# Second layer in three sets instead of two, expert results added on VectorE, one product for features and logits, all orders written anew

## The reference, cut to what matters

```python
# layer 0
f = xn @ W.T + b                                  # features, per batch of 256 tokens
e = f @ f.T + distance_bias;  s = softmax(e) @ f
shared = (silu(xn @ Sg.T) * (xn @ Su.T)) @ Sd.T
probs = sigmoid(xn @ router.T + routing_bias)     # 8 experts, the best 2 per token, weights normalised
g = shared + sum over 2 experts of weight * ((silu(xn @ G[e]) * (xn @ U[e])) @ D[e])
x = x + s * silu(g)
# layer 1
w = xn @ Wqkv.T, 16 heads of 8;  w_normed = w / norm over tokens
Pi = softmax over heads(sum(w_normed^2) * temp);  dots = sum over tokens(Pi_norm * w * w)
s = -(w * Pi / (1 + dots)) @ Wout.T + bout
expert of a batch = argmax(softmax(gelu(last token @ Wp1 + bp1) @ Wp2 + bp2))
g = xn + 0.3 * ((gelu(xn @ W1[sel] + b1) @ W2[sel] + b2) @ Wo + bo)
x = x + s * silu(g)
```

## Time and profile before

| | |
|---|---|
| median of 3 runs | 431.0 us (427.37 to 431.69) |
| profiled execution, span | 338.1 us |
| around the span (median less span) | 92.9 us |
| TensorE busy | 312.5 us, 92% of the span |
| TensorE weight loads | 259.6 us, 77% |
| VectorE busy | 208.9 us, 62% |
| ScalarE busy | 206.7 us, 61% |
| POOL busy | 138.5 us, 41% |
| bytes moved | 31.91 MB, mean 94 GB/s |

### The profile page before, as it was taken

One profiled execution on the slowest core, in us unless ns is written; L12 is line 12 of the kernel. 1 busy time (PEld: TensorE's weight loads), 2 busy tenths in 40 slices (PEclk: granted clock), 3 DMA queues, 4 the chain that ended last, 5 costly groups with the idle time before them and its releaser, 6 DMA issues.

```text
span 338.1 us, 7770 instructions
## 1 busy us (share of the span) xinstructions
PE 312.5 (92%) x2077; PEld 259.6 (77%) x2077; DVE 208.9 (62%) x779; ACT 206.7 (61%) x504; POOL 138.5 (41%) x152
## 2 busy tenths in 40 slices
PE   7879999999999799999998899898879999989994
PEld 6657555669999799999988767688854588768793
DVE  4999792225776765556544457665365848578465
ACT  2296754348776666565654435674586768897772
POOL 2200577777777746666664434454540000000000
PEclk9999999999999999999999999999997999999999
DMA  6980023113431113333333721111006532017403
GB/s 187 294 367 4 32 66 104 56 49 87 105 95 57 48 33 89 94 92 87 103 94 108 261 65 35 55 33 33 31 7 244 120 77 57 3 32 211 133 17 109
DMA packets 29321, 31.91 MB, mean 94 GB/s; under 512 B 7120, under 2 KB 22610, under 8 KB 29152
## 3 DMA queue, kind: packets, MB, share of 16 engines
q1 hardware_dynamic: 24960, 22.97, 24.1%
q0 software_dynamic: 4320, 8.47, 7.5%
HBM read 19.86 MB, written 12.01 MB: 94 GB/s over the span
## 4 chain that ended last, share of the span: by engine, by line
PE 72%; DVE 11%; ACT 5%; issue 5%; SPq 2%; DMA 2%; DVEq 1%; ACTq 0%
PE PS L474 19%; PE PS L486 9%; PE PS L414 4%; PE PS L690 3%; PE PS L401 3%; PE PS L440 3%; PE PS L698 3%; PE PS L626 2%; PE PS L390 2%; PE PS L392 2%; PE PS L627 2%; PE PS L642 2%; PE PS L628 2%; DVE XA L924 2%; PE PS L454 2%
## 5 line engine op out<-in xcount | busy, mean ns | idle before, releaser
L2010 POOL DMA_INDIRECT yc_scratch<-YS,XS x71 | 71.6, 1009 | 61.1 <-ACT YS L1609 44.6
L474 PE MATMUL PS<-XG,XT 128*128 128x128 f32 x568 | 76.7, 278 | 6.9 <-issue 3.0
L474 PEld LDWEIGHTS PS<-XG,XT 128*128 128x128 f32 x568 | 69.0, 192 | 10.1 <-issue 6.3
L1126 DVE COPY XT<-WE 128x512 f32 x71 | 30.9, 435 | 38.5 <-issue 21.3
L1602 ACT ACTIVATE EP<-PS 128x256 f32<-128x256 f32 x71 | 27.0, 383 | 43.3 <-PE PS L474 42.3
L486 PE MATMUL PS<-WE,EP 128*128 x284 | 43.9, 278 | 1.9 <-ACT YS L1609 1.8
L2001 POOL DMA_INDIRECT xs_scratch<-XA,POS x32 | 31.4, 981 | 29.9 <-DVE POS L1035 20.5
L486 PEld LDWEIGHTS PS<-WE,EP 128*128 128x128 f32 x284 | 37.6, 191 | 5.9 <-issue 5.9
L1117 DVE TENSOR_TENSOR EP<-EP,PS 128x256 f32<-128x256 f32 x71 | 29.6, 417 | 18.4 <-PE PS L486 15.9
L2001 POOL DMA_INDIRECT xs_scratch<-XB,POS x32 | 31.2, 976 | 9.8 <-issue 9.8
L1609 ACT ACTIVATE YS<-PS,XS 128x128 f32<-128x128 f32 x71 | 26.0, 366 | 5.2 <-PE PS L486 2.0
(11 more groups left out here) (190 smaller groups left out, 601.3 us busy)
## 6 DMA issues: line engine op xcount, KB each, us to landing
XS<-xs_scratch SPq DMA_DIRECT2D x71, 65.0 KB, 1.9
XB<-yc_scratch SPq DMA_DIRECT2D x16, 256.0 KB, 4.4
S<-in_w SPq DMA_DIRECT2D x13, 256.0 KB, 2.6
WE<-in_we SPq DMA_DIRECT2D x1, 3072.0 KB, 14.8
X<-in_x SPq DMA_DIRECT2D x16, 128.0 KB, 3.0
out<-X SPq DMA_DIRECT2D x16, 128.0 KB, 1.8
yc_scratch<-YS,XS POOLq DMA_INDIRECT x71, 2.3
SH<-in_w SPq DMA_DIRECT2D x3, 256.0 KB, 2.5
```

Source lines behind the costliest of these rows:

```text
L474: m = e.matmul(PS[k][:, f * 128:(f + 1) * 128], WC[:, u % 4, f * 128:(f + 1) * 128], XG[:, g % 2, j * 128:(j + 1) * 128], start=True, stop ...
L1126: e.tensor_copy(WC[:, u % 4, :], WE[:, bass.ds(r, 512)]).then_inc(s_wc, 1)
L2010: e.indirect_dma_start(out=yc, out_offset=bass.IndirectOffsetOnAxis(ap=XS[:, g % 4, j, 128:129].bitcast(U32), axis=0), in_=YS[:, u % 8, :] ...
```

## The change

It does six things.

1. **Routing and sets.** Group 0 is three chunks instead of four (CA = 3). The units come in three sets, for chunks 0 to 2, 3 to 5 and 6 to 7 (SETS = 0, 3, 6, 8), with a table of five runs of eight experts instead of three. The number of units stays 71. Results are collected chunk by chunk in one transfer each, and the experts of layer 1 are chosen in three sets.
2. **Results on VectorE.** `add_up` goes. `add_results` adds the two results of a chunk into F, `add_shared` adds the shared output; `gated` then reads and writes F.
3. **Features and logits in one product.** `project`, `logits` and `bias` go. `features` multiplies XT of each tile (as weights) with W and the router side by side, 136 columns; VectorE adds both biases at once into F. `turn_f` transposes F to FT.
4. **Banks per product.** Every helper of TensorE gets its bank and the semaphore value that frees it as arguments, call by call.
5. **Buffers.** HHE gets its own memory, layer 1's transposed input goes to the memory of SH (X1T), H1 and PXP to XT's.
6. **All orders anew.** The lists of SyncE, TensorE, VectorE and ScalarE are different throughout. Units 0 and 1 now start before most of the attention of layer 0; mix(13) to (15) come between units 38 and 48, layer 1 of the first set from unit 38 on. The loads of x and the stores are one transfer per chunk instead of two, and the first fetch waits for the empty rows' blocks too.

```diff
-CA = 4
+CA = 3
 NTS = (4 * CA, NT - 4 * CA)
-FULL = 8 * CA - 7
-DONE = 8 * CA + 7
-BESIDE = 36
+SETS = (0, 3, 6, 8)
+FULL = 8 * SETS[1] - 7
+DONES = (8 * SETS[1] + 7, 8 * SETS[2] + 7, NU)
...
+                if u == 0:
+                    e.wait_ge(s_experts, 1)
+                    e.wait_ge(d_fill, 16 * (NE + 1))
+                    e.wait_ge(d_disp[0], 16 * 2 * NTS[0])
+                if u == FULL:
+                    e.wait_ge(d_disp[1], 16 * 2 * NTS[1])
...
+            def collect(c):
+                if c in SETS:
+
+                    last = DONES[set_of(c)]
+                    for u in range(last - 8, last):
+                        e.wait_ge(d_y[u % 8], 16 * (u // 8 + 1))
+                if c >= 3:
+                    e.wait_ge(s_ya, c - 2)
+                e.dma_start(YC[:, 4 * (c % 3):4 * (c % 3) + 4, :, :].rearrange("p (b t) s d -> p b (t s d)", b=2),
+                            yc.rearrange("(c b p q) d -> c p b (q d)", c=NC, b=2, q=4)[c]).then_inc(d_yt[c], 16)
...
+            def features(b, k, free=None, n=0):
+
+                e.wait_ge(s_xt, b // 2 + 1)
+                if b == 0:
                     e.wait_ge(d_wa, 16)
-                for t in range(4 * c, 4 * c + 4):
-                    m = e.matmul(PS[(2, 7)[g]][:, 8 * t:8 * t + 8], tile(XT, t), a_("router"), start=True, stop=True)
...
+                when(free, n)
+                for i in range(2):
+                    m = e.matmul(PS[k][:, i * 136:(i + 1) * 136], tile(XT, 2 * b + i), WA[:, 0:136], start=True, stop=True)
+                m.then_inc(p_fl, 1)
...
-            def gate_up(u):
+            def gate_up(u, k, free=None, n=0):
                 g, j = divmod(u, 4)
-                k = u % 3 if u < BESIDE else u % 2
...
-                if u >= BESIDE:
-                    e.wait_ge(s_hhe, u - 1)
...
-            def down_e(u):
-                k = (5, 7)[u % 2] if u < BESIDE else 5
+            def down_e(u, k, free=None, n=0):
                 e.wait_ge(s_hhe, u + 1)
-                if u == 0:
-                    e.wait_ge(s_s, NB)
-                elif u >= 2:
-                    e.wait_ge(s_ys, u - 1 if u < BESIDE else u)
+                when(free, n)
...
-                e.matmul(quarters(k), ident, four(SH, c), start=True, stop=False)
-                e.matmul(quarters(k), ident, results(c, 0), start=False, stop=False)
-                e.matmul(quarters(k), ident, results(c, 1), start=False, stop=True).then_inc(p_acc, 1)
...
+            def add_results(c):
+                e.wait_ge(d_yt[c], 16)
+                e.wait_ge(p_mix, 2 * c + 2)
+                e.tensor_tensor(four(F, c), results(c, 0), results(c, 1), ALU.add).then_inc(s_ya, 1)
+
+            def add_shared(c):
+                e.wait_ge(s_sh, c + 1)
+                e.wait_ge(s_ya, c + 1)
+                e.tensor_tensor(four(F, c), four(F, c), four(SH, c), ALU.add).then_inc(s_acc, 1)
...
+            def features(b, k):
+                e.wait_ge(p_fl, b + 1)
+                if b == 0:
+                    e.wait_ge(d_wa, 16)
+                e.tensor_tensor(F[:, 2 * b:2 * b + 2, :], PS[k][:, 0:272].rearrange("p (i d) -> p i d", i=2),
+                                a_("bias").unsqueeze(1).broadcast_to([128, 2, 136]), ALU.add).then_inc(s_f, 1)
```

More of the change, by code:

```diff
@@ L42 @@
 CW, _c = {}, 0
-for _n, _w in [("ident", 128), ("one", 1), ("upper", 128), ("e8", 256), ("unit", 1), ("head", 16), ("lb", 25), ("next", 24), ("dist", 512)]:
+for _n, _w in [("ident", 128), ("one", 1), ("upper", 128), ("e8", 256), ("unit", 1), ("head", 16), ("lb", 41), ("next", 40), ("whole", 24), ("dist", 512)]:
     CW[_n] = (_c, _c + _w)
@@ L47 @@
 AW, _c = {}, 0
-for _n, _w in [("w0", 128), ("router", 8), ("rbias", 8), ("b0", 1)]:
+for _n, _w in [("w0", 128), ("router", 8), ("bias", 136)]:
     AW[_n] = (_c, _c + _w)
@@ new lines, in _ @@
+            for i in range(NE):
+                end = e.value_load(CI[0:1, i:i + 1])
+                e.dma_start(xs[bass.ds(end, 128), :], ZB[:, :]).then_inc(d_fill, 16)
+            fetch(0)
+            fetch(1)
+            fetch(2)
+            fetch(3)
+            fetch(4)
+            fetch(5)
+            fetch(6)
+            fetch(7)
+            fetch(8)
+            fetch(9)
+            fetch(10)
+            fetch(11)
+            fetch(12)
+            fetch(13)
+            fetch(14)
@@ L295, in _ @@
+            fetch(37)
+            fetch(38)
+            fetch(39)
+            fetch(40)
+            fetch(41)
+            fetch(42)
+            fetch(43)
+            fetch(44)
+            fetch(45)
             collect(0)
-            for u in range(DONE + 16, NU):
-                fetch(u)
             collect(1)
+            collect(2)
+            fetch(46)
+            fetch(47)
+            fetch(48)
+            fetch(49)
+            fetch(50)
+            fetch(51)
+            fetch(52)
@@ new lines, in experts @@
+                a1, f2, rows = (whole[:, 8 * i:8 * i + 8] for i in range(3))
+                whole1, one1, whole2, one2, rest = (size[:, 8 * i:8 * i + 8] for i in range(5))
+                start1, start2, start3, start4 = (first[:, 8 * i:8 * i + 8] for i in range(1, 5))
+                left, b1, m2, ahead, left2, cap, done = spare[0:7]
+                e.tensor_tensor(left, rows, a1, ALU.subtract).then_inc(s_vec, v.up())
+                e.tensor_copy(whole1, a1).then_inc(s_vec, v.up())
+                e.tensor_tensor(start1, start1, a1, ALU.add).then_inc(s_vec, v.up())
```

2425 lines of the change are left out of this document (1353 added, 1072 removed).

## The result

The kernel after takes **402.4 us** (median of four runs, 400.37 to 403.96); the kernel before took 429.2 us beside it (four runs, 426.42 to 431.69). The ratio is 0.938, with a 95% interval of 0.932 to 0.943: 26.7 us less, where 404.5 us was forecast. The number came out right. The picture behind it did not, and the first view of the profile says so. The profiled execution has a span of 400.7 us and a time of 402.5 us: there are 1.8 us around the span, not 92.9. The missing time lies inside the span.

The account below looks back on a forecast made before the run. The prediction took TensorE to bound the kernel nearly everywhere; savings of 20.6 us (add-ups) and 5.9 us (projection and router) made 26.5, so 431.0 - 26.5 = 404.5 us, own range 398 to 416, overall range 391 to 429.

Parts of the forecast that it names:

- The time around the span: Whole run: the 92.9 us between the profiled span of 338.1 and the median of 431.0 stay untouched.
- TensorE sets the time nearly everywhere: Whole kernel: TensorE, busy 312.5 of 338.1 us, is the bound; it idles only 25.6 us.
- Term 1: Add-ups of eight chunks: 24 products of 512 columns at 0.86 us leave TensorE for VectorE, saving 20.6 us.
- Term 2: Projection and router: products of 6.9 and 6.5 us give way to 136-column ones of 7.5, net saving 5.9 us.
- TensorE busy, about 286 forecast: Whole kernel: a sign of the forecast, TensorE's busy time falling from 312.5 to about 286 us.
- Units 8 to 39 are the same work at 1.45 us: Expert units 8 to 39: same work, each unit keeping its price of 1.45 us.
- ScalarE becomes the bound: Units 43 to 66: ScalarE needs 50 us against TensorE's 42, so TensorE idles some 8 us.
- rival B: ScalarE's 16 added table loads show in full, 20.5 us come back: 425 us; chance 0.21.
- rival C: Units 43 to 66 and tail: each pair of table loads costs TensorE 4 us, 32 in all: 436.5 us; chance 0.11.
- Rival A: From 170 us on: banks per product end ring waits, 13.6 us more gained: 391 us; chance 0.18.
- Dispatch and TensorE arrive together, near 115 to 120: Start to unit 8: dispatch's end and TensorE meet near 115 to 120 us, no gain beyond 5.9 us, no loss.
- SyncE's orders: Last group, units 68 to 70: new transfers ahead of fetch(68) and fetch(70) cost nothing; a late choice would hold three units.

Follow-up runs that it names:

- experiment 5: The kernel after with the dispatch's 64 indirect transfers made plain ones to fixed places, still issued by POOL, rows not sorted by expert: 341.5 us.
- experiment 1: The kernel before, unchanged, profiled once more: 426.2 us, the profiled execution with a span of 426.8 us.
- experiment 3: The kernel before with only the add-up moved from TensorE to VectorE: 424.3 us against 430.1, ratio 0.987.
- experiment 4: The kernel after with a waited-for memset on POOL behind each of the 64 dispatch transfers, 2.1 us apart: 388.6 us, ratio 0.907.
- experiment 2: The kernel after, unchanged, profiled once more: 404.35 us, ratio 0.944, span 402.9 us.
- experiment 12: The kernel after with memset-spaced indirect transfers, scatters of units 0 to 5 woven into dispatch(1), and down_e(u-2) behind gate_up(u) for units 9 to 38: 365.2 us.
- experiment 8: The kernel after with silu in place of layer 1's square root, exp and gelu, 11 table loads instead of 40: 403.5 us, ratio 0.945.
- experiment 7: The kernel after with a memset behind every indirect transfer and scatters of units 0 to 7 woven into dispatch(1): 374.7 us, ratio 0.884.
- experiment 10: The kernel before with a POOL memset behind each of its 135 indirect transfers, 1.46 us apart: 399.3 us, ratio 0.931.

## Why the prediction was right, and where it was not

**The time around the span: wrong.** "I take the 92.9 us between them as untouched" was the largest number in the forecast and was no time around the span. It was a standstill of the first layer, missing in the one execution read. The sum held since both kernels have it, at 90 and 94 us. A span of 338.1 against runs of 431.0 is itself the finding: the execution that was read is not the one that was timed. "TensorE sets the time nearly everywhere" holds only behind 138 us. And the 26.5 us were counted where they do not appear. With the standstill the change gives 26.1 us of span; without it, as far as experiment 5 stands for that, nothing. Cut at the first gate products of unit 9 and unit 39 and at the last one:

| stretch | before, first execution | after, experiment 5 | before, experiment 1 | after |
|---|---|---|---|---|
| start to unit 9 | 129.5 | 133.3 | 204.5 | 191.9 |
| units 9 to 38 | 44.5 | 61.5 | 56.0 | 61.5 |
| unit 39 to the last gate product | 68.9 | 73.4 | 70.6 | 71.9 |
| tail | 95.2 | 73.2 | 95.7 | 75.4 |
| span | 338.1 | 341.4 | 426.8 | 400.7 |

The first pair has no standstill, the second has one. (Experiment 5 has plain transfers, so its start is not quite the kernel's own.) The tail gains 20 to 22 us in both. The units lose 17 us without the standstill and 5.5 with it, since the kernel before is slower there too. The first layer gains 12.6 us only with it.

**Term 1, add-ups, 20.6 us: right in size, wrong in path.** The first four are 6 us (experiment 3), less than the 10.3 forecast. The other four covered a wait for the experts' biases and were worth nothing alone; with the choice in three sets that wait is gone, and the tail came out at 75.4 us instead of 95.7. The prediction named this wait ("the waits for weights and the idle after the last product stay") and had it backwards: the whole change took away its cover and the wait with it.

**Term 2, products of 136 columns: right.** Eight passes in an unbroken row take 0.93 us start to start, 0.116 us a pass, where 0.117 was taken (timeline of TensorE in experiment 4, from one row of eight to the next product):

```profile
40.82 1.09 PE L431 MATMUL PS<-WA,XT 128*128 128x136 f32 x8
41.75 1.02 PE L463 MATMUL PS<-XT,WB 128*128 128x512 f32 x2
```

The median of the 64 passes is 0.116 us in the kernel after too. So the net saving of 5.9 us stands as a price.

**TensorE busy, about 286 forecast, 313.2 measured.** One part is the standstill, in which products run at half clock: before has 329.9 with it and 312.5 without. Without a standstill (experiment 5) the kernel after has 305.8. The saving of 26.5 became about 7, and the next point is why: among units 9 to 38 TensorE is busy 53.3 us in experiment 5 and 44.4 in the kernel before's first execution, for the same products.

**"Units 8 to 39 are the same work at 1.45 us": the step that failed.** The work is the same, its order is not. Before, `down_e(u)` stands two `gate_up` behind its own; after, one. Silu and the product on VectorE are 0.38 and 0.41 us, and the handovers between three engines come on top; that does not fit into the 0.89 us of one `gate_up`. In the kernel after TensorE waits for hidden in 19 places, 13.0 us. And a wait costs more than it shows (timeline of TensorE in the kernel after, then in the first execution of the kernel before):

```profile
193.35 1.10 PE L521 MATMUL PS<-XG,XT 128*128 128x128 f32 x8
195.09 0.91 PE L529 MATMUL PS<-WE,HHE 128*128 x4 [0.64 <-DVE HHE L1251]
196.02 1.13 PE L521 MATMUL PS<-XG,XT 128*128 128x128 f32 x8
```
```profile
138.44 1.06 PE L474 MATMUL PS<-XG,XT 128*128 128x128 f32 x8
139.33 0.61 PE L486 MATMUL PS<-WE,EP 128*128 x4
139.78 1.06 PE L474 MATMUL PS<-XG,XT 128*128 128x128 f32 x8
```

One gate group and one down product take 2.67 us start to start above and 1.34 below: 1.33 us more, of which the profile calls 0.64 idle. The rest stands in the products' own times, so it is counted as busy. Units 9 to 38 take 2.05 us each in the kernel after and also in experiment 5 (2.16 in experiment 2), against 1.48 in the first execution of the kernel before. But that 1.48 was no price of the timed runs: in experiment 1 the kernel before itself needs 1.87. So the two orders differ by 0.57 us a unit without a standstill, but only by 0.18 to 0.29 with one, and with the old distance put back (experiment 12) it is 1.85 from unit 15 on. The list of calls showed this before any run; I read it for table loads and for banks, not for the distance between a product and its consumer. Why the kernel before needs 1.87 with the standstill and 1.48 without, long after it, is open.

**ScalarE and VectorE: right.** 40 table loads, 216.7 us (222 forecast); VectorE 222.6 (229 forecast), the bias additions 0.430 us (0.42 to 0.44), the additions 0.68 (0.69). Units 43 to 66 came out at the length forecast, 51.6 us (262.0 to 313.6) for 50, but not by ScalarE: it is busy 42.0 of them, and "ScalarE becomes the bound" is wrong. TensorE waits there 2.2 us for hidden and for no eviction, and experiment 8 took 29 loads away without effect. Hence **rival B** and **rival C** fall. As to the price of a load, in the earlier trace rows the next function starts 20 ns behind it, and before the eight loads of the gates (L1875) ScalarE idles 0.1 us in all. The Trainium skill ("ScalarE: Activation LUTs", What ACT_TABLE_LOAD costs) adds a drain of about 1380 ns to each load; these traces show none. By the Trainium skill's 2.66 us for a switch 29 loads fewer would have freed 77 us of ScalarE, an estimate. The time did not move, so the forecast of 447 us falls with rival C whatever the drain is.

**Rival A, the banks:** 2.1 us for twelve units in the kernel before; the stage after isn't above 95% busy (units 43 to 66: 47.4 of 51.6 us, 92%; all units: 130.0 of 147.3, 88%).

**"Dispatch and TensorE arrive together, near 115 to 120": wrong.** Dispatch ends at 131.8, beyond the 125 us that the prediction had named as a sign, and 17.4 us of that is POOL waiting for positions(1), which VectorE, having stood still, delivers at 80.2; in experiment 5 they are there at 62.1. SyncE's orders: no wait of TensorE in the tail is for a transfer, so nothing shows a cost, as taken. The last unit's gate product, forecast near 230, comes at 325.3, and at 268.2 in experiment 5; part of the tail's work now stands before it.

So the sum was wrong in three places that cancel: the units gave 5.5 us back where the first four add-ups (10.3) should have shown, and layer 0 (11.3 us less up to the steady units, where 5.9 was booked) and the tail (20.3, where 10.3 was booked) gave more. Why layer 0 gave 11.3 was not taken apart; it is where the standstill lies. That the forecast fell about 2 us from the median is luck: the 26.5 us of work are off TensorE, but the time that they should have freed came from elsewhere.

## What to carry to other kernels

Set the span of the profiled execution against the time of the timed runs first. Here they lie 1.8 us apart when profile and time are of one execution, and lay 92.9 apart when they were not alike; take another profile then, before any sum is made. A forecast of a difference can come true on a wrong base, so check it stage by stage. When lists of calls are rewritten, count for each product how many others stand between it and the one that consumes its result, and compare that with the chain of engines between them; idle time shows only about half of what a missed handover cost here. Before booking work taken off a path as gain, look for the wait that it covered.

## What the runs showed of the hardware

Long rows of indirect transfers issued by POOL 1.27 us apart can bring TensorE, VectorE, ScalarE and SyncE nearly to a stop: TensorE is busy 26 of 90 us in the kernel before (experiment 1) and 33 of 94 in the kernel after, and SyncE needs 54.0 and 15.2 us for the eight transfers of the empty rows that took 8.1 in the execution without a standstill, with POOL itself undisturbed. At 1.46 us apart the pieces are up to 3.9 us (experiment 7), 9.9 (experiment 12) or 15.3 (experiment 10); at 2.1 there are none, and twelve scatters at 1.27 us in the same execution bring them back (experiment 4). Plain transfers 0.54 us apart by the same engine do nothing of the kind. One execution of the kernel before, with the same 64 transfers at 1.27 us, had no standstill; what makes the difference was not found, and neither was what the engines wait for.
